# Row maxima rounded once and q and k spread in pairs of groups, in a twelve-stage transformer kernel

## The reference, cut to what matters

```
scores = einsum('bhqd,bhkd->bhqk', Q, K) / sqrt(dk)
scores = where(causal, scores, NEG)
m = max(scores, axis=-1, keepdims=True)
e = exp(scores - m)
out = einsum('bhqk,bhkd->bhqd', e / sum(e), V)
```

## Time and profile before

| | us |
|---|---|
| median of 3 runs | 3336.43 |
| lowest and highest | 3324.67, 3341.25 |
| span of the profiled execution | 3337.4 |
| PE busy | 2641.8 (79%) |
| ACT busy | 1912.7 (57%) |
| DVE busy | 1763.9 (53%) |
| mean granted clock of TensorE | 0.795 of full |

### The profile page before, as it was taken

One profiled execution on the slowest core, in us unless ns is written; L12 is line 12 of the kernel. 1 busy time (PEld: TensorE's weight loads), 2 busy tenths in 40 slices (PEclk: granted clock), 3 DMA queues, 4 the chain that ended last, 5 costly groups with the idle time before them and its releaser, 6 DMA issues.

```text
span 3337.4 us, 46425 instructions
## 1 busy us (share of the span) xinstructions
PE 2641.8 (79%) x18736; PEld 1529.0 (46%) x18736; DVE 1763.9 (53%) x2698; ACT 1912.7 (57%) x1960; POOL 3.6 (0%) x12
## 2 busy tenths in 40 slices
PE   8999999777997789877898688986889868897215
PEld 4666456343563435534355344553445534453102
DVE  5463574545656355553555545654455544563524
ACT  2433435875358753586445864468534685447994
POOL 0000000000000000000000000000000000000000
PEclk7997989659896588966899668986779867987557
DMA  3000000000000000000000000000000000000000
GB/s 128 2 1 1 20 1 1 1 1 8 1 1 1 1 8 1 1 1 0 8 1 1 1 0 8 2 1 1 0 5 2 1 1 0 4 1 1 0 0 6
DMA packets 4561, 18.68 MB, mean 6 GB/s; under 512 B 608, under 2 KB 864, under 8 KB 3808
## 3 DMA queue, kind: packets, MB, share of 16 engines
q1 hardware_dynamic: 4320, 15.38, 1.2%
HBM read 13.28 MB, written 2.10 MB: 5 GB/s over the span
## 4 chain that ended last, share of the span: by engine, by line
PE 54%; ACT 19%; DVE 15%; issue 12%; DVEq 0%; DMA 0%; ACTq 0%; SPq 0%
ACT back_cosines L1320 6%; PE one_ps L1164 2%; PE two_ps L1275 2%; PE one_ps L862 2%; PE two_ps L910 2%; ACT back_cosines L1322 2%; PE one_ps L1710 2%; DVE back_nsum L1330 2%; PE one_ps L1717 2%; ACT L1320 2%; PE one_ps L766 1%; PE one_ps L1723 1%; DVE back_cosines L1393 1%; ACT L1862 1%; PE two_ps L862 1%
## 5 line engine op out<-in xcount | busy, mean ns | idle before, releaser
L1320 ACT ACTIVATE back_cosines<-back_cosines 128x2048 f32<-128x2048 f32 x256 | 472.2, 1899 | 0.5
L933 ACT ACTIVATE front_scratch<-one_ps 128x1152 f32<-128x1152 f32 x168 | 171.5, 1021 | 225.0 <-PE one_ps L848 224.8
L1322 ACT ACTIVATE back_cosines<-back_cosines,wts 128x2048 f32<-128x2048 f32 x128 | 252.4, 1994 | 41.1 <-DVE back_cosines L1393 40.9
L1330 DVE TENSOR_REDUCE back_nsum<-back_cosines 128x8 f32<-128x2048 f32 x64 | 144.4, 2281 | 234.0 <-ACT back_cosines L1320 234.0
L797 DVE TENSOR_REDUCE front_negm<-one_ps 128x8 f32<-128x1024 f32 (+1 forms) x168 | 204.4, 1220 | 56.6 <-PE one_ps L772 55.5
L837 PE MATMUL one_ps<-ident_bf,mask_q 128*128 128x256 bf16 x480 | 93.3, 302 | 80.5 <-ACT front_scratch L933 69.3
L696 ACT ACTIVATE back_cosines<-two_ps,wts 128x512 fp32r<-128x512 f32 x28 | 19.3, 688 | 224.1 <-PE two_ps L910 224.1
L766 PE MATMUL one_ps<-front_qkr 32*128 32x128 f32 (+1 forms) x896 | 136.5, 414 | 14.1 <-issue 8.9
L1393 DVE TENSOR_SCALAR back_cosines<-two_ps 128x2048 f32<-128x2048 f32 x56 | 128.2, 2290 | 28.5 <-PE two_ps L1257 28.3
L933 ACT ACTIVATE back_cosines<-two_ps 128x1152 f32<-128x1152 f32 (+1 forms) x84 | 86.0, 1024 | 92.0 <-PE two_ps L848 92.0
L766 PEld LDWEIGHTS one_ps<-front_qkr 32*128 32x128 f32 x896 | 96.6, 274 | 88.5 <-DVE front_negm L797 46.3
(11 more groups left out here) (630 smaller groups left out, 5795.1 us busy)
## 6 DMA issues: line engine op xcount, KB each, us to landing
wts<-w_dram SPq DMA_DIRECT2D x1, 4184.0 KB, 15.3
front_xin<-x_dram SPq DMA_DIRECT2D x8, 256.0 KB, 4.2
out_dram<-back_z SPq DMA_DIRECT2D x8, 256.0 KB, 2.1
wts<-w_dram SPq DMA_DIRECT2D x1, 1736.5 KB, 19.1
wts<-w_dram SPq DMA_DIRECT2D x1, 1199.0 KB, 5.3
wts<-w_dram SPq DMA_DIRECT2D x1, 1152.0 KB, 16.5
wts<-w_dram SPq DMA_DIRECT2D x3, 256.0 KB, 5.8
wts<-w_dram SPq DMA_DIRECT2D x1, 516.5 KB, 4.8
```

The costliest lines, as they stand in the source:

```text
L933: nc.scalar.activation(h.probs[:, e % 2, 0:n * HEADW].rearrange("p (k c) -> p k c", c=HEADW), h.ps[:, 0:n, 0:HEADW], ACT.Exp, scale=float( ...
L1320: nc.scalar.activation(cosines, cosines, func, scale=scale).then_inc(h.arc_pass.sem, 1)
L1322: nc.scalar.activation(cosines, cosines, func, scale=scale, bias=C(bias)).then_inc(h.arc_pass.sem, 1)
L1330: nc.vector.tensor_reduce(h.nsum[:, kt, :].rearrange("p (g2 j) -> p j g2", g2=2), h.cosines[:, u % 2, kt * 4 * TOK:(kt + 1) * 4 * TOK].rea ...
```

## The change

Row maxima are rounded once. negm becomes an fp32r tensor, so that the reduction (797, 1200) writes rounded maxima into the first of the two columns, and the second stays zero (max_columns gives the first alone). The four copies of line 805, the signed rounding and the remainder (700 and 704 for maxTr) go. The four transposes become ordinary matmuls with an fp32r identity, ident_r. Three of the tiles wait for all sets but the last and go to one bank, the fourth waits for the last set and goes to the next bank. DVE copies 384 columns and then 128 columns of them to maxTr. mqa does the same.

q and k of causal stages are spread in pairs. q is projected into bank 2, k into 0, v into 1. Groups 0 and 1 are spread into banks 2 and 3, groups 2 and 3 into banks 0 and 1, each pair in a step with four matmuls. q's first pair waits for q's two parts alone. DVE now takes the first pair (banks 2 and 3), ACT the second. k's first pair waits for DVE's copy of q's first pair, k's second for ACT's copy of q's second.

The maxima begin with the first pair. The sets of the first sequence come in another order, so that set 0 needs groups 0 and 1 alone and uses banks 2 and 3. It waits for the first pair of q and k, and set 1 for the rest.

The tables are new. PE_RUNS goes from 190, 154 and 147 entries to 204, 165 and 160, ACT_RUNS from 88, 104 and 121 to 118, 133 and 130, DVE_RUNS from 104, 116 and 115 to 150, 131 and 136. linear, arccos and the other stages have the same instructions.

```diff
-    b, part, js = m // 6, m // 2 % 3, slice(2 * (m % 2), 2 * (m % 2) + 2)
+    b, part, first = m // 6, MPARTS[m // 6][m // 2 % 3], 2 - 2 * (m % 2)
+    js = slice(first, first + 2)
...
+def spread_pairs_pe(pe, h, turn, s):
+    yield
+    pe.wait_ge(h.q_split.sem, h.q_split.at(turn, s, 2))
+    if s in TWICE:
+        pe.wait_ge(h.norm_out.sem, h.norm_out.at(turn, s, 2))
+    spread_pair_pe(h, 0, ("q_of_high", "q_of_low"), 0, h.q_ps)
+    yield
+    pe.wait_ge(h.k_split.sem, h.k_split.at(turn, s, 2))
+    pe.wait_ge(h.v_ready.sem, h.v_ready.at(turn, s))
+    spread_pair_pe(h, 0, ("q_of_high", "q_of_low"), 1, h.q_ps)
+    yield
+    pe.wait_ge(h.q_outer.sem, h.q_outer.at(turn, s))
+    spread_pair_pe(h, 2, ("k_of_high", "k_of_low"), 0, h.k_ps)
+    yield
+    pe.wait_ge(h.q_ready.sem, h.q_ready.at(turn, s))
+    spread_pair_pe(h, 2, ("k_of_high", "k_of_low"), 1, h.k_ps)
+
+def spread_pair_pe(h, first, tables, pair, done):
+    for i, table in enumerate(tables):
+        for g, bank in zip((2 * pair, 2 * pair + 1), PAIR_BANKS[pair]):
+            last = nc.tensor.matmul(h.ps[:, bank, :], picks[table][rows(g, QUAD), :], halves_of(h, first + i)[rows(g, QUAD), :],
+                                    start=(i == 0), stop=(i == 1), skip_group_check=True)
+    last.then_inc(done.sem, 1)
...
+def max_end_pe(pe, h, turn, s, sets, bank):
+    yield
+    pe.wait_ge(h.max_done.sem, h.max_done.at(turn, s, sets - 1))
     for t in range(TILES):
-        last = nc.tensor.transpose(h.ps[:, 0, t * P:(t + 1) * P], h.negm[:, t, :], C("ident"))
-    last.then_inc(h.negm_ps.sem, 1)
+        if t == TILES - 1:
+            yield
+            pe.wait_ge(h.max_done.sem, h.max_done.at(turn, s, sets))
+        last = nc.tensor.matmul(h.ps[:, bank + t // (TILES - 1), t % (TILES - 1) * P:(t % (TILES - 1) + 1) * P],
+                                h.negm[:, t, :], ident_r[:], start=True, stop=True, skip_group_check=True)
+        if t >= TILES - 2:
+            last.then_inc(h.negm_ps.sem, 1)
...
-    for t in range(TILES):
-        last = nc.vector.tensor_copy(max_columns(h, slice(t, t + 1), 1)[:, 0], max_columns(h, slice(t, t + 1), 0)[:, 0])
-    last.then_inc(h.max_pair.sem, 1)
-    high_dve(dve, h.ps[:, 0, :], h.high[:, 0, :], "m_sign", h.negm_high)
-    split_dve(dve, h.ps[:, 0, :], h.high[:, 0, :], "m_low", h.maxTr[:, :], h.negm_ready)
+def max_end_dve(dve, h, turn, s, bank):
+    for i, columns in enumerate((slice(0, (TILES - 1) * P), slice((TILES - 1) * P, TOK))):
+        yield
+        dve.wait_ge(h.negm_ps.sem, h.negm_ps.at(turn, s, i + 1))
+        nc.vector.tensor_copy(h.maxTr[:, columns], h.ps[:, bank + i, 0:columns.stop - columns.start]).then_inc(h.negm_ready.sem, 1)
```

More of the change, by code:

```diff
@@ L665, in headed_project_pe @@
                 last.then_inc(h.k_ps.sem, 1)
+            if s in CAUSAL:
+                yield from spread_pairs_pe(pe, h, turn, s)
+                return
             yield
@@ L724, in headed_project_act @@
                 yield
-                act.wait_ge(ps_sig.sem, ps_sig.at(turn, s, 3 if s == "linear" and ps_sig is h.k_ps else 2))
-                nc.scalar.activation(into[:, 0:2, :], h.ps[:, 0:2, :], ACT.Copy).then_inc(ready.sem, 1)
+                if s in CAUSAL:
+                    act.wait_ge(ps_sig.sem, ps_sig.at(turn, s, 3))
+                    nc.scalar.activation(into[:, 2:4, :], h.ps[:, 0:2, :], ACT.Copy).then_inc(ready.sem, 1)
+                else:
+                    act.wait_ge(ps_sig.sem, ps_sig.at(turn, s, 3 if ps_sig is h.k_ps else 2))
+                    nc.scalar.activation(into[:, 0:2, :], h.ps[:, 0:2, :], ACT.Copy).then_inc(ready.sem, 1)
         def headed_project_dve(dve, h, turn, s):
@@ L1128, in mqa_pe @@
                         last.then_inc(h.max_ps.sem, 1)
-            yield
-            pe.wait_ge(h.max_pair.sem, h.max_pair.at(turn, s))
-            for t in range(TILES):
-                last = nc.tensor.transpose(h.ps[:, 0, t * P:(t + 1) * P], h.negm[:, t, :], C("ident"))
-            last.then_inc(h.negm_ps.sem, 1)
+            yield from max_end_pe(pe, h, turn, s, 2 * TILES, 0)
             for e in range(QSETS + 1):
```

102 lines of the change are left out of this document (52 added, 50 removed), and 80 rows, old and new, of tables (ACT_RUNS, DVE_RUNS, PE_RUNS).

## The result

The changed kernel takes 3318.28 us (median of 10 runs, 3310.64 to 3327.03) where the kernel before takes 3337.61 (10 runs beside them, 3324.67 to 3351.97). The ratio is 0.994, with a 95% interval of 0.9922 to 0.9958: 0.6% faster, 19 us. Forecast were 30 us (3307).

The account below looks back on a forecast made before the run. No engine alone bounds the kernel: in the loop DVE, PE and ACT each bound different stretches. Gains of 14 + 3 + 10 + 3 + 3 + 3 = 36 us less a price of 6 give 30 us, 3307 us (3290 to 3325).

Parts of the forecast that it names:

- The size of the short end: End of causal and mqa maxima: scores begin 1.0 us after the last reduction instead of 3.25, saving 2.2 us a stage.
- step (1): Maxima's ends, nearly all in the loop's causal1 and mqa: of 28 us less PE idle, half, 14 us, comes back.
- Step (2): Spreads, where PE waits 17.7 us for DVE's copy of q: 6 us go, by half 3 us gained.
- Step (3): Causal0 of the loop, DVE the bound: first maxima 1.6 us earlier come back whole, 6 x 1.6 = 10 us.
- The price of the pairs: PE in causal spreads: 0.4 us a stage, between nothing and 1.5; 16 x 0.4 = 6 us lost.
- Step (5): Fronts and backs: a third of the front chain's 9.8 us, 3 us gained; in the backs another 3.
- Nothing comes back: Rival, chance 0.18: ACT holds its two loop stretches, only causal0's gain less the pairs' price stays: 3333 us.
- Everything comes back: Rival, chance 0.22: the front's chain is the longest in each pass and new tables turn its 9.8 us into time: 3271 us.
- The third: Rival, chance 0.17: 20 us a pass of PE-bound causal0 scores and moe0 fall to the low clock, costing 65 us: 3372 us.

Follow-up runs that it names:

- e2: Kernel before with only the maxima rounded once and the short end of the maxima, whole spreads, old order: 3337.28 us, ratio 1.0012.
- e6: Kernel before with only the changed kernel's order tables (empty steps where they count more), neither edit: 3375.28 us, ratio 1.0113.
- e5: Changed kernel with its new tables and pairs, but the old end of the maxima: 3358.50 us, ratio 1.0068.
- e3: Kernel before with only the spreads in pairs and maxima begun with the first pair, old end, old order: 3351.03 us, ratio 1.0035.
- e7: Changed kernel with its new tables and maxima rounded once, but q and k spread whole: 3337.41 us, ratio 0.9998.
- e4: Changed kernel with only its fronts in the order of the kernel before, steps joined there: 3315.91 us, ratio 0.9935.
- e8: e4 with all four groups of q and of k spread at once in the fronts: 3309.07 us, ratio 0.9920; again 3309.49 us, 0.9888.
- e10: e8 with the fronts' maxima in the order of the kernel before: 3299.81 us, ratio 0.9877.
- e1: Changed kernel, both edits, with the kernel before's order tables and joined steps: 3340.28 us, ratio 1.0025.
- e9: e8 with ACT's copy of k's second pair moved ahead of two arccos activations in the loop's causal1: 3319.66 us, ratio 0.9913.

## Why the prediction was right, and where it was not

The sign and the range held, and 30 us were forecast for 19 (28.6 between the profiles). That the total came near is partly luck: by the profiles the loop gave 13 us more than its terms, the fronts 14 less, and the two misses cancel:

| part | forecast | between the profiles |
|---|---|---|
| fronts | 3 gained, 1.6 lost to pairs | 12.8 lost |
| loop | 14 + 3 + 10 + 3 gained, 4.8 lost to pairs | 38.3 gained |
| backs | 3 gained | 3.1 gained |

**The size of the short end** was right in each of its terms: 0.92 us for 1.0; two copies of 384 and 128 columns in 0.94 for 0.92; reductions as long in the new format (1.23 against 1.22). The line of the new matmuls, which answers to the earlier trace rows (duration min/median/max in ns):

```profile
L831 PE MATMUL one_ps<-ident_r,front_negm x84: 273/415/667, 51.1 to 2736.5; 128*128 128x128 f32 x84
L831 PE MATMUL two_ps<-ident_r,back_negm x28: 273/302/329, 503.6 to 2930.3; 128*128 128x128 f32 x28
```

A matmul takes 415 ns at the low clock where a transpose took 421, and 302 at the full one where it took 273. The Trainium skill, Perfetto Trace Analysis, section Transposes, would have a logical transpose not be a standard matmul; at this tile the rows show nothing for its rule at the low clock and at most 0.03 us a tile at the full one, and three of four are hidden here.

**What the short end brings back, step (1),** was half of 28 us, with "only what new tables can move behind it". That it hangs on the tables was right: with the old ones it brings nothing (e2: 2.34 us shorter, 2.31 us more wait behind it). But the term gave to the short end what the order brings. In causal1, mqa and moe1 of the loop a pass lost 4.6 us (234.4 to 229.8), 28 over six, the whole of the term. The order without an edit has 2.5 of the 4.6 (e6), and it is the order that puts one activation in place of two ahead of causal1's first exponential; how much of the 2.5 hangs on that was not measured. The short end, added to order and pairs (e5 to the changed kernel), has 0.9, some 5 us over six and no more than the spread of such profiles. What it is worth in the new order in all, 1.3%, came by the profiles from the fronts and from causal0 and moe0, where the sum gave it 3 us at most. Why there stays open.

**Step (2), the spreads' wait,** was to give 3 us. Nothing of it is seen: the wait is 20.4 us for 17.7, and set 1 of causal1's maxima waits 17.5 us more.

**Step (3), causal0's 1.6 us, failed.** It said that DVE is the bound there and that 1.6 us come back whole. The timeline of the changed kernel, which answers to the earlier trace rows:

```profile
828.63 1.03 ACT L750 ACTIVATE one_v<-one_ps 128x1024 f32<-128x1024 f32 x1 [0.29 <-PE one_ps L653]
...
829.09 0.39 PE L710 MATMUL one_ps<-front_split_parts,picks_q_of_high 32*128 32x512 f32 x2
829.32 0.40 PE L710 MATMUL one_ps<-front_split_parts,picks_q_of_low 32*128 32x512 f32 x2
829.33 1.23 DVE L787 CAST back_qkr<-two_ps 128x1024 fp32r<-128x1024 f32 x1 [0.27 <-PE two_ps L719]
...
830.47 1.22 DVE L784 CAST front_qkr<-one_ps 128x1024 fp32r<-128x1024 f32 x1
...
831.60 1.22 DVE L787 CAST back_qkr<-two_ps 128x1024 fp32r<-128x1024 f32 x1
831.74 0.51 PE L710 MATMUL one_ps<-front_split_parts,picks_k_of_high 32*128 32x512 f32 x4 [0.38 <-DVE front_qkr L784]
832.08 0.40 PE L710 MATMUL one_ps<-front_split_parts,picks_k_of_low 32*128 32x512 f32 x4
...
832.74 1.22 DVE L784 CAST front_qkr<-one_ps 128x1024 fp32r<-128x1024 f32 x1
...
834.10 0.50 PE L812 MATMUL one_ps<-front_qkr 32*128 32x256 f32 x4
```

q's first pair is spread at 829.09, before v is done (829.66), as forecast. But DVE takes the other half's copy (L787) at 829.33 and the front's at 830.47, and so on in turn: four copies of 1.22 us stand one behind the other from 829.33 to 833.96. From v to the first maxima it is 4.44 us (829.66 to 834.10), where it was 4.46, and it is the same within 0.03 us in all six passes of both kernels. The step had the evidence against it in its own row: DVE is busy 10.00 of 10 us there. On a bound engine an earlier start of one copy only changes the turn; time would have come back if DVE had less to do, and the pairs take no copy from it.

**The price of the pairs,** 0.4 us a stage between 0 and 1.5, shows in the same rows. A pair by itself keeps PE 0.63 us (829.09 to 829.72), and q's two pairs take 1.35 (829.09 to 830.44) where the eight of k, issued together, take 0.74 (831.74 to 832.48). So a spread whose pairs stand apart costs 0.6 us more, one whose pairs meet nothing. The Trainium skill, TensorE: Matmul & The Clock Gate, section Measured speedup vs the span model, has by its span model two row tiles take about as long as four; the trace agrees for pairs that are issued apart. In time the pairs cost 0.35% with the old order (e3), and with the new one and the short end they bring 0.6% (e7 against the changed kernel).

**Step (5), the fronts, failed in its sign.** It looked only at the chain, and forgot that new tables order the fronts too. e4 gave 8.2 of the 12.8 us back with the old order there, e8 3.5 more with whole spreads, e10 5 more with the maxima as they were, each within the spread of single profiles, all three together (16.7 us) twice as much. In the fronts both halves run the same stages with little slack (33 us of idle PE in all), and ACT is busy for only 145 of 422 us, so the queue in which the loop's gain was found is not full there. That this is the reason is argued, not shown; that the order loses there is shown by e6 too (440.0 against 408.9 with no edit at all).

**The rivals.** "Nothing comes back" is what the edits do without the order (e1, e2). "Everything comes back" did not happen, as step (3) and the fronts show. The third, a fall of the clock in 120 us of PE-bound work of a pass, did not happen either: causal0's scores took 45.7 us at 1.00 in every pass, before and after, and the loop's mean clock went from 0.79 to 0.81. But in five of six passes the clock was lower where the text had not looked, in causal0's maxima, which is the last section.

## What to carry to other kernels

Where two streams of work share in-order queues, a shortened chain is worth what the next queue releases: follow it past its end to the first wait for another engine, and if that engine is busy without a pause, the gain goes into that wait (e2, e9). A fine order and the edits for which it was made can each be worthless or harmful alone and gain together, so they have to be tested crosswise, and stretch by stretch: here one stretch gained by the order alone while others lost, and undoing most of the change in the fronts (e10) brought the gain from 0.6% to 1.2%, measured in another set of runs. And before single profiles are compared, the same code has to be profiled more than once: here its stretches differed by as much as the change is worth.

## What the runs showed that was not expected

The mean granted clock over one and the same piece of code differs from pass to pass. Windows over causal0's maxima in two passes of one execution of the changed kernel (columns as in the earlier trace rows):

```profile
433.90:463.10 29.20, 25.70 (x278) 15.53 (x277) 25.82 (x30) 2.06 (x3) 0.00 (x0) 0.82 0.01 1
834.10:868.90 34.80, 33.95 (x278) 19.67 (x277) 26.22 (x30) 2.06 (x3) 0.00 (x0) 0.56 0.00 1
```

The same 278 matmuls take 29.2 us at a mean granted clock of 0.82, and 34.8 at 0.56; DVE is as busy in both. In the kernel before, where 253 matmuls fall into this stretch, it was 32.1 us at 0.63 in five of six passes, and once 37.0 at 0.51:

```profile
829.80:861.90 32.10, 28.57 (x253) 16.20 (x252) 25.47 (x28) 2.06 (x3) 0.00 (x0) 0.63 0.00 1
2466.10:2503.10 37.00, 33.70 (x253) 18.70 (x252) 25.92 (x28) 2.06 (x3) 0.00 (x0) 0.51 0.00 1
```

The kernel of e8, run twice, had five passes with 28.2 to 30.6 us and one with 34.7 in the first profile (six passes in 2408.2 us), and one with 29.2 and five with 34.7 to 35.9 in the second (2432.1 us). That is 24 us between two executions of one program, more than the change itself is worth in the median, and the six stretches of maxima hold all of it (180.9 us in the first, 205.6 in the second). The profile of the changed kernel had one pass of six at the quicker level, the one of before none. The second pass, whose stages are compared at the top, was at 0.56 in the one and 0.63 in the other, with 34.8 us of maxima for 32.1, and its 2.2 us more in causal0 come with that; how much of them is the clock and how much the 25 matmuls more is not told apart. Over six passes causal0's maxima took 197.7 us before and 204.6 in the changed kernel, so the loop gained in spite of them. What decides the level in a pass no run here tells; no kernel was made to vary it.
